# Projection behind the first layer of a four-layer graph network: two PSUM banks in turn, transposes ahead, low part taken later

## What is computed

```python
def _layernorm(x, axis=-1, eps=1e-5):
    m = jnp.mean(x, axis=axis, keepdims=True)
    v = jnp.var(x, axis=axis, keepdims=True)
    return (x - m) / jnp.sqrt(v + eps)

# layer 0: eight attention heads, their outputs joined in `out`
return jax.nn.relu(out)                       # (out has the biases in it)

# layer 1
H_ = jnp.einsum('nd,hde->hne', H, W)          # the projection of this stage
out = jnp.einsum('nm,hme->hne', adj, H_) + b[:, None, :]

x = _layernorm(x + _L0_gnn_ref(x, adj, ...), axis=-1)
x = _layernorm(x + _L1_gnn_ref(x, adj, L1_gnn_W, L1_gnn_b), axis=-1)
```

## Time and profile before

| | |
|---|---|
| median of three runs | 3566.08 us (3560.08 to 3570.93) |
| profiled execution, whole time | 3560.0 us |
| profiled execution, span | 3558.2 us |
| TensorE busy | 3160.6 us (89%) |
| VectorE busy | 2328.3 us (65%) |
| ScalarE busy | 1715.9 us (48%) |
| stage of the change | first VectorE work at 987.44 us, last end at 1109.20 us |

### The profile page before, as it was taken

The page is one execution under the profiler, slowest core; times in us unless marked ns, Lnnn a source line. Parts: engine busy times, 40 slices in busy tenths (PEclk is TensorE's granted clock), DMA queues, the critical chain, the costliest instruction groups (busy, mean ns, idle before and its releaser), DMA issues. The chain is left out here.

```text
span 3558.2 us, 35485 instructions
## 1 busy us (share of the span) xinstructions
PE 3160.6 (89%) x13715; PEld 2212.1 (62%) x13715; DVE 2328.3 (65%) x3070; ACT 1715.9 (48%) x1553; POOL 255.4 (7%) x441
## 2 busy tenths in 40 slices
PE   5799999999977999975888885999999876999994
PEld 4533333333334777754777774888888736888883
DVE  5599999999864665655666645888888552122226
ACT  0299999999811211113333426888888412000002
POOL 0000000000011111110000000010101000000003
PEclk9999999999998999997999997999999988999997
DMA  7500000000033676666222217676767424766654
GB/s 284 209 17 9 16 16 10 13 15 15 0 107 132 246 273 244 246 224 230 96 98 101 101 68 294 239 282 243 277 244 276 194 72 174 317 272 272 272 201 130
DMA packets 119286, 580.90 MB, mean 163 GB/s; under 512 B 13376, under 2 KB 21795, under 8 KB 95312
## 3 DMA queue, kind: packets, MB, share of 16 engines
q1 hardware_dynamic: 96528, 443.44, 32.8%
q0 software_dynamic: 22592, 135.19, 10.5%
HBM read 374.87 MB, written 203.71 MB: 163 GB/s over the span
## 5 line engine op out<-in xcount | busy, mean ns | idle before, releaser
L516 PE MATMUL bank<-dist,hf 128*65 128x512 f32 (+2 forms) x2112 | 805.1, 543 | 12.4 <-ACT dist L478 12.4
L516 PEld LDWEIGHTS bank<-dist,hf 128*65 128x65 f32 x2112 | 290.6, 138 | 519.0 <-issue 484.2
L1378 PE MATMUL bank<-pt,HA 128*128 128x256 f32 x1936 | 505.1, 381 | 4.5 <-DMA HA<-features 4.5
L478 ACT ACTIVATE dist<-dist 128x1408 f32<-128x1408 f32 (+1 forms) x352 | 452.9, 1322 | 4.6
L1567 PE MATMUL bank<-w,EM 128*128 128x256 f32 x1936 | 426.0, 380 | 12.3 <-DMA w<-weights 12.3
L1567 PEld LDWEIGHTS bank<-w,EM 128*128 128x128 f32 x1936 | 369.3, 191 | 62.6 <-DMA w<-weights 12.5
L1378 PEld LDWEIGHTS bank<-pt,HA 128*128 128x128 f32 x1936 | 328.7, 191 | 28.0 <-DMA HA<-features 4.7
L409 DVE TENSOR_TENSOR dist<-msk,sB 128x1408 f32<-128x1408 uint8 (+1 forms) x208 | 324.9, 1562 | 23.5 <-PE bank L516 13.8
L1366 PE MATMUL bank<-idt,v 128*128 128x128 f32 x1936 | 302.3, 277 | 40.9 <-ACT v L1252 33.6
L1305 DVE COPY pt<-bank 128x512 f32<-128x512 f32 (+1 forms) x440 | 264.4, 630 | 112.5 <-PE bank L1366 110.6
L469 ACT ACTIVATE dist<-dist,neg_t 128x1408 f32<-128x1408 f32 (+1 forms) x208 | 295.1, 1419 | 60.2 <-DVE dist L409 56.9
(11 more groups left out here) (162 smaller groups left out, 4437.8 us busy)
## 6 DMA issues: line engine op xcount, KB each, us to landing
w<-weights SPq DMA_DIRECT2D x44, 2816.0 KB, 9.8
weights<-pt SPq DMA_DIRECT2D x220, 512.0 KB, 3.8
al<-in_adj_cols SPq DMA_DIRECT2D x22, 1408.0 KB, 8.1
at<-in_adj_tiles SPq DMA_DIRECT2D x22, 1408.0 KB, 8.2
rows<-in_adj_rows SPq DMA_DIRECT2D x22, 1408.0 KB, 6.5
HB<-in_adj_rows POOLq DMA_DIRECT2D x22, 1354.0 KB, 7.6
rows_low<-HB POOLq DMA_DIRECT2D x22, 1354.0 KB, 6.0
rows<-rows_low POOLq DMA_DIRECT2D x22, 1354.0 KB, 8.3
```

The lines of the kernel that those rows point to most:

```text
L478: act.activation(d[:, 0:VALID[c]], d[:, 0:VALID[c]], ACT.Exp, scale=-1.0).then_inc(p_ready, 1)
L516: mm = pe.matmul(sums_bank(hh, k)[0:FW, 0:hi - a * P], hf[hh][:, m, :], d[:, a * P:hi], start=(m == 0), stop=(m == T - 1))
L1378: t = pe.matmul(acc_t[n % 2][:, 0:P2], HA[:, m, h * D3:(h + 1) * D3], pt[n % 2][:, m, :, :].rearrange("p r n -> p (r n)"), start=(m == 0), ...
```

## The change

The products of tile j go to bank `into[j % 2]`, that is `pj` and `sc` in turn. TensorE runs the transposes of tile j+1 ahead of the products of tile j, and waits ahead of the products of tile j for the low part of tile j-2 instead of j-1. ScalarE copies the transposed tile j and then the high part of tile j-1. VectorE takes the low part of tile j-2 between the moments of tile j and the write of its normed tile; the last two low parts come behind the loop. To allow this the first half of `ln_tile` becomes a function `ln_moments`; in other stages `ln_tile` issues what it did before. SyncE's and GpSimd's programs are the same. `normed` goes, its instructions now stand in the loop.

```diff
--- before.py
+++ after.py
@@ -164,8 +164,7 @@
             act.wait_ge(rows_turned, n)
             act.activation(rows_sb[0:width, :], etp[0:width, 0:128], ACT.Copy).then_inc(rows_out, 1)
 
-        def ln_tile(dve, n, q, R, st, xn):
-
+        def ln_moments(dve, n, q, R, st):
             dve.wait_ge(r_full, n + 1)
             dve.bn_stats(st[q][:, 0:6], R[q][:, :]).then_inc(ln_stats, 1)
             carry(dve, set_const, 1)
@@ -173,6 +172,9 @@
             dve.bn_aggr(st[q][:, 6:8], st[q][:, 0:6]).then_inc(ln_mean, 1)
             dve.wait_ge(ln_mean, n + 1)
             dve.tensor_scalar(st[q][:, 8:9], st[q][:, 7:8], LN_EPS, None, ALU.add).then_inc(ln_var, 1)
+
+        def ln_tile(dve, n, q, R, st, xn):
+            ln_moments(dve, n, q, R, st)
             dve.wait_ge(ln_rstd, n + 1)
 
         def ln_write(dve, n, q, R, st, dst):
@@ -540,20 +542,13 @@
             pool.wait_ge(ln_done, n + 1)
             pool.dma_start(dst[2 * i + q], xn[q][:, :]).then_inc(xn_stored[q], 16)
 
-        def normed(dve, n, i, q, R, st, xn, phase):
-            ln_tile(dve, n, q, R, st, xn)
-            wait(dve, xn_stored[q], 16 * (phase * PAIRS + i))
-            wait(dve, turned, n + T - 1)
-            ln_write(dve, n, q, R, st, xn[q][:, :])
-
-
-
         L1 = ExitStack()
         HR, HL = sb(L1, "HR", [P, T, D], F32R), sb(L1, "HL", [P, T, D], F32R)
         h_hi = sem("h_hi")
         with ExitStack() as ph:
             R, xn, st, xin, xt, bias, w_sb = norm_buffers(ph)
             c_in = sem("e0_in")
+            into = (pj, sc)
             with nc.Block() as block:
                 @block.sync
                 def _(sp):
@@ -570,23 +565,26 @@
                 def _(dve):
                     dve.wait_ge(c_in, 32)
 
-                    def body(i):
-                        for q in (0, 1):
-                            j = 2 * i + q
-                            dve.tensor_tensor(R[q][:, :], HB[0:P, j, :], bias[:, :], ALU.add).then_inc(r_half, 1)
-                            dve.wait_ge(r_half, j + 1)
-                            dve.wait_ge(x_in[q], 16 * (PAIRS + i + 1))
-                            dve.scalar_tensor_tensor(out=R[q][:, :], in0=R[q][:, :], scalar=0.0, in1=xin[q][:, :],
-                                                     op0=ALU.max, op1=ALU.add).then_inc(r_full, 1)
-                            normed(dve, j, i, q, R, st, xn, 0)
-                            if not (isinstance(i, int) and j == 0):
-                                h_out(j - 1)
-
                     def h_out(j):
                         dve.wait_ge(h_hi, j + 1)
-                        dve.tensor_tensor(HL[:, j, :], pj[0:P, :], HR[:, j, :].bitcast(FP32), ALU.subtract)\
+                        dve.tensor_tensor(HL[:, j, :], into[j % 2][0:P, :], HR[:, j, :].bitcast(FP32), ALU.subtract)\
                            .then_inc(proj_out, 1)
-                    pair_loop(dve, body, first=True)
+
+                    for j in range(T):
+                        q = j % 2
+                        dve.tensor_tensor(R[q][:, :], HB[0:P, j, :], bias[:, :], ALU.add).then_inc(r_half, 1)
+                        dve.wait_ge(r_half, j + 1)
+                        dve.wait_ge(x_in[q], 16 * (PAIRS + j // 2 + 1))
+                        dve.scalar_tensor_tensor(out=R[q][:, :], in0=R[q][:, :], scalar=0.0, in1=xin[q][:, :],
+                                                 op0=ALU.max, op1=ALU.add).then_inc(r_full, 1)
+                        ln_moments(dve, j, q, R, st)
+                        if j >= 2:
+                            h_out(j - 2)
+                        dve.wait_ge(ln_rstd, j + 1)
+                        wait(dve, xn_stored[q], 16 * (j // 2))
+                        wait(dve, turned, T + j - 1)
+                        ln_write(dve, j, q, R, st, xn[q][:, :])
+                    h_out(T - 2)
                     h_out(T - 1)
 
                 @block.gpsimd
@@ -602,23 +600,32 @@
                 def _(pe):
                     pe.wait_ge(c_in, 32)
 
-                    def body(i):
-                        for q in (0, 1):
-                            j = 2 * i + q
-                            pe.wait_ge(ln_done, j + 1)
-                            turn_tile(pe, T + j, xn[q])
-                            project(pe, T + j, xt[q], w_sb, (D,))
-                    pair_loop(pe, body)
+                    def turn_next(j):
+                        pe.wait_ge(ln_done, j + 1)
+                        turn_tile(pe, T + j, xn[j % 2])
+
+                    turn_next(0)
+                    for j in range(T):
+                        if j + 1 < T:
+                            turn_next(j + 1)
+                        pe.wait_ge(turned_out, T + j + 1)
+                        wait(pe, proj_out, T + j - 1)
+                        for k in range(KT):
+                            t = pe.matmul(into[j % 2][0:P, :], xt[j % 2][:, k, :], w_sb[:, k, :],
+                                          start=(k == 0), stop=(k == KT - 1))
+                        t.then_inc(proj_mm, 1)
 
                 @block.scalar
                 def _(act):
-                    def body(i):
-                        for q in (0, 1):
-                            j = 2 * i + q
-                            keep_turned(act, T + j, xt[q])
-                            act.wait_ge(proj_mm, T + j + 1)
-                            act.activation(HR[:, j, :], pj[0:P, :], ACT.Copy).then_inc(h_hi, 1)
-                    pair_loop(act, body)
+                    def high(j):
+                        act.wait_ge(proj_mm, T + j + 1)
+                        act.activation(HR[:, j, :], into[j % 2][0:P, :], ACT.Copy).then_inc(h_hi, 1)
+
+                    for j in range(T):
+                        keep_turned(act, T + j, xt[j % 2])
+                        if j > 0:
+                            high(j - 1)
+                    high(T - 1)
 
 
         with ExitStack() as ph:
```

## The result

| | median of 17 runs | profiled span |
|---|---|---|
| before | 3565.62 us | 3558.2 us |
| changed | 3581.76 us | 3576.4 us |

The ratio is 1.0047, 95% interval 1.0036 to 1.0059: the changed kernel is 16.1 us slower by the medians. The forecast was 3583 us.

What follows compares the result with a forecast made beforehand. A chain from engine to engine bound the stage; 20 periods each 0.79 us longer, with a later start and the end, made it 17.0 us longer: 3566.1 us becomes 3583 us, range 3576 to 3600.

Steps and rivals of the forecast that it cites:

- The chain: Projection stage, each tile: products, high part, low part, write, transposes run in series; period 5.97 us against 5.18, 0.79 more.
- gap: TensorE's idle time from products' end to the next transposes, each period: 1.88 us instead of 0.84.
- The two unknown terms: In each period: low part's start to write 0.61 us (0.72 if it waits for the end); transposes to products 0.42.
- The start: First products of the stage wait behind the second transposes: start 996.01 instead of 993.19, take 5.98 us again.
- The end: Stage's last products follow after about 3.5 us without transposes; from their start to the last low part's end 5.03.
- The costs put at nothing: Projection stage: GpSimd's power and the DMA loads on SP's queue were claimed to cost nothing.
- Rival 1: Projection stage: idle gaps let TensorE's clock fall, 5.5 falls, +9.3 us, 3592 us; range 3588 to 3600; chance 0.35.
- Rival 2: Projection stage: the chain doesn't close, TensorE runs without a gap; about -20 us, 3546 us; chance 0.03.
- Rival 3: Projection stage: more overlap or earlier write, period grows only 0.2 to 0.3; +5 to +8, 3573 us; chance 0.05.
- the 0.84: Products' idle wait for the low part in front, per tile in us, claimed removed by alternating two banks.
- The clock and the transposes: Projection stage: transposes count as work for the clock, so the gap is 1.88 us, not 2.30.

Runs made afterwards that it cites:

- three tiles back: Changed kernel with VectorE taking the low part of tile j-3, not j-2, between moments and write: 3541.64 us, ratio 0.9933.

## Why the prediction was right

- **The chain.** The step that carried it, write(j+1) behind low part(j-1) behind products(j-1), with transposes(j+1) waiting for that write, held in every link. Forecast period 5.97, measured 5.96; gap 1.88, measured 1.87. The two unknown terms came out as taken: write start 0.60 behind the low part's start (forecast 0.61, and not 0.72), and products 0.49 behind the transposes' start (forecast 0.42). This last was 0.07 short, and the products' own time is 3.60 where I took 3.67: the two cancel.
- **The start.** Forecast: first products 2.82 later and again 5.98 long. They started 998.15 - 989.56 = 8.59 behind the first residual sum, before 993.19 - 987.44 = 5.75, so 2.84 later. But they took 4.61, as the clock rose sooner after their start: in the first 5 us from it the mean granted clock was 0.80, before it was 0.54. That is 1.4 of the 1.6 us by which the stage's 17.0 was too much (15.4 measured). The second execution of the changed kernel had 0.50 and 6.15 us there, and its stage is 17.0 longer than before (138.7 against 121.8). So this term varies from one execution to the next by more than the forecast missed by, and a hit to 1 us in the whole time is in part luck. A view of the same stretch in the first execution:

```profile
998.00:1003.00 5.00, 4.76 (x10) 1.91 (x8) 1.54 (x4) 0.80 (x2) 0.65 (x2) 0.78 0.32 108
```

- **The end.** The last two products took 7.03 together, and from there to the end of the last low part is as forecast: 1126.73 - 1118.34 = 8.39, against 3.5 + 5.03 = 8.53.
- **The costs put at nothing** were nothing: the power on GpSimd was done 1.6 us before the low part started, SP's loads don't appear among the stage's waits, and a whole addition of 0.61 us ahead of the low part cost nothing.
- **Rival 1** did not come, but its chance rested on a wrong reading. I took 1.88 as "just under" the gaps of 2.10 that fell in 3 of 11 tiles, and 5.5 falls as its middle. At 1.97 there were 9, near the end of its range that I had called one at every other gap. Layer 2 idles once in some 23 us, this stage once in 6, and a share of gaps doesn't carry over between them. The forecast stood 0.10 us from a time 15 us longer: that the clock held at 1.87 was not worked out from any row, and was luck.
- **Rival 2** asked for an index read wrongly, and was excluded rightly; its time of 3546 us is what the kernel takes when the index is another (3541.6 us, TensorE with no gap, 3.88 us a tile). The period of 4.0 worked out for it was nearly right. Rival 3 did not come: the period grew by 0.78 us, not by 0.2 to 0.3.
- **What I didn't see** in the rows of before: that two waits of 0.85 and 0.79 stood side by side, so that the banks alone bring nothing, although the prediction writes down the 0.84 as removed and says that the transposes and their copy cost nothing. The timeline has both ends, 1052.27 and 1052.21; the wait's name has one. It changed no term of the sum.
- **The clock and the transposes.** That transposes count as work for the clock rests on the earlier trace rows still; no run here separates it further, since a gap with the transposes added would be 0.49 longer in each of the kernels alike. The Trainium skill, page "TensorE: Matmul & The Clock Gate", section "A second HAM failure mode: psum-queue depth-cycling", describes what was seen at 1.97 and more, a clock that goes to and fro between groups of matmuls with short idle times; here it came with the idle time and not with the banks, since three tiles back uses the same two banks at a granted clock of 1.00.

## What to carry to other kernels

When one engine works ahead, count the lag of every later step from that engine's place in its own list and not from the loop index of the engine that does the step: "two tiles back" was no tile back for TensorE, and one index more turned 16 us of loss (ratio 1.0047) into some 24 us of gain (0.9933). Before removing a wait, look in the timeline for the end of every other input of the waiting instruction; the second one may be 0.06 us shorter, and its own chain may run over two tiles. In a closed chain a short instruction costs by its place alone: the same addition was free ahead of the wait and 15 us behind it.

## What the runs showed of the hardware

Behind gaps in TensorE's work that return each 6 to 6.6 us the granted clock fell in none of 20 at 1.87 us (in three executions), in nine at 1.97 us, worth 1.69 us each, and in only three at 2.47 us, worth 1.5 us each. VectorE starts an independent instruction 0.08 to 0.09 us before the reported end of the one in front (1051.11 + 0.69 = 1051.80 against 1051.71; 1040.70 + 0.68 against 1041.30), in the first case with waits for three semaphores between them that were met. Eight records of products took 3.60 us right behind transposes and 3.67 to 3.70 behind a wait; what makes the 0.07 wasn't tried.
